# Router logits with the tokens as the stationary operand, in both mixtures of experts

## The reference

```python
# first mixture: 8 experts, top 2, and a gated shared expert
logits = jnp.einsum('bsh,eh->bse', x, gate_w)
probs = jax.nn.softmax(logits, axis=-1)
top_w, top_i = jax.lax.top_k(probs, K)
top_w = top_w / jnp.sum(top_w, axis=-1, keepdims=True)
...
shared_gate = jax.nn.sigmoid(x @ shared_gate_w)
...
# second mixture: 16 experts, top 6 of probs + gate_b
scores = xf @ gate_w.T
probs = jax.nn.softmax(scores.astype(jnp.float32), axis=-1)
biased = probs + gate_b
_, idx = jax.lax.top_k(biased, TOP_K)
```

## Time and profile before

| | |
|---|---|
| Time, median of 3 runs | 2141.92 us (2141.73 to 2150.73) |
| Span of the profiled execution, first to last instruction | 2139.0 us |
| Profiled execution's own time | 2139.0 us within its span; what lies around the span isn't shown |
| TensorE matmuls busy | 2077.7 us (97%), 12193 matmuls |
| VectorE busy | 1455.7 us (68%) |
| ScalarE busy | 1221.1 us (57%) |
| GpSimd busy | 576.8 us (27%) |

### The profile page before, as it was taken

How to read it: one execution, slowest core, us unless ns; L and a number is a source line. 1 busy time by engine, 2 the same in 40 slices (tenths; PEclk the granted TensorE clock), 3 DMA queues, 4 the chain that set the end, 5 groups by cost and what they waited for, 6 DMA issues and landing times. The chain is left out here.

```text
span 2139.0 us, 33422 instructions
## 1 busy us (share of the span) xinstructions
PE 2077.7 (97%) x12193; PEld 1588.5 (74%) x12193; DVE 1455.7 (68%) x2761; ACT 1221.1 (57%) x2435; POOL 576.8 (27%) x679
## 2 busy tenths in 40 slices
PE   8999999999999999989999999999999999999997
PEld 6888888888788888877777765333334688778886
DVE  5666666677667666666656567999994557655555
ACT  5666666666556666554444335888887434444433
POOL 3444444444334444332221110000000112222221
PEclk9999999999999999999999999999999999999999
DMA  2000000000000000011111202100000111111111
GB/s 75 20 21 18 16 21 21 21 21 21 9 21 21 21 21 20 4 38 45 38 44 40 56 22 44 24 19 22 21 12 1 43 37 45 45 45 45 45 52 57
DMA packets 55143, 64.67 MB, mean 30 GB/s; under 512 B 10268, under 2 KB 35655, under 8 KB 54983
## 3 DMA queue, kind: packets, MB, share of 16 engines
q1 hardware_dynamic: 54982, 62.55, 10.5%
HBM read 52.42 MB, written 2.10 MB: 25 GB/s over the span
## 5 line engine op out<-in xcount | busy, mean ns | idle before, releaser
L868 POOL TENSOR_TENSOR a_pr<-a_pr,a_rinv 128x512 f32<-128x512 f32 (+3 forms) x384 | 312.2, 827 | 474.7 <-DVE a_rinv L1118 474.7
L86 PE MATMUL psum<-xh,g_hi_gu 128*128 128x512 f32 x920 | 375.5, 408 | 7.8 <-DVE f_hid L1612 6.3
L88 PE MATMUL psum<-xh,g_lo_gu 128*128 128x512 f32 x920 | 359.8, 391 | 0.0
L87 PE MATMUL psum<-xl,g_hi_gu 128*128 128x512 f32 x920 | 359.2, 390 | 0.0
L1208 POOL TENSOR_TENSOR g_lo_gu<-g_raw_gu,g_hi_gu 128x512 fp32r<-128x512 f32 x84 | 108.8, 1295 | 758.5 <-ACT g_hi_gu L1204 758.5
L1926 ACT ACTIVATE a_pt<-psum 128x512 f32<-128x512 f32 x512 | 276.2, 597 | 59.2 <-PE psum L1826 37.9
L1945 DVE TENSOR_REDUCE x_m_negm<-psum 128x1 f32<-128x1024 f32 x240 | 290.8, 1224 | 13.5 <-PE psum L1811 11.2
L1546 ACT ACTIVATE f_act_s<-psum,g_gu_bias 128x512 f32<-128x512 f32 (+1 forms) x168 | 115.1, 685 | 295.5 <-PE psum L88 295.3
L1625 DVE TENSOR_TENSOR f_hl<-f_hid,f_hh 128x512 fp32r<-128x512 f32 x164 | 115.6, 705 | 226.3 <-ACT f_hh L1558 224.6
L1023 ACT ACTIVATE a_pr<-psum,a_negm 128x128 f32<-128x128 f32 (+7 forms) x256 | 190.1, 742 | 107.0 <-DVE a_negm L1108 102.9
L1030 ACT ACTIVATE a_pth<-psum 128x512 fp32r<-128x512 f32 (+3 forms) x384 | 174.7, 489 | 113.1 <-PE psum L927 107.7
(11 more groups left out here) (316 smaller groups left out, 4302.3 us busy)
## 6 DMA issues: line engine op xcount, KB each, us to landing
g_raw_gu<-in_gu SPq DMA_DIRECT2D x82, 256.0 KB, 2.8
f_raw_dn<-in_down SPq DMA_DIRECT2D x82, 128.0 KB, 2.0
g_raw_gu<-in_qkv SPq DMA_DIRECT2D x32, 256.0 KB, 2.8
a_wvr<-in_qkv SPq DMA_DIRECT2D x32, 128.0 KB, 2.4
a_wor<-in_o SPq DMA_DIRECT2D x32, 128.0 KB, 2.0
x_queries_qq<-x_qhi SPq DMA_DIRECT2D x128, 32.0 KB, 1.9
yT<-in_xT SPq DMA_DIRECT2D x4, 512.0 KB, 6.6
x_queries_qq<-x_qlo SPq DMA_DIRECT2D x64, 32.0 KB, 1.9
```

What stands on the lines that cost most here:

```text
L86: pe.matmul(out, a_hi, b_hi, start=first, stop=False)
L87: pe.matmul(out, a_hi, b_lo, start=False, stop=False)
L88: return pe.matmul(out, a_lo, b_hi, start=False, stop=last)
L868: pool.tensor_tensor(x, x, rinv[:, j:j + 1].to_broadcast([P, count * P]), ALU.mult).then_inc(p_done, 1)
```

## The change

The operands of `lg` are swapped: for each tile of 128 tokens the tokens are the stationary operand and the 10 or 16 columns of router weights move. The result has the tokens on the partitions, so the transposes of `lt`, its two copies' target in `yT` and the task itself go away. VectorE copies each `lg` task's four tiles straight into `lg`, and after the second it goes on with the maximum and the subtraction. The lists of tasks lose one entry for each router and, where slots are counted, the pause behind it.

```diff
     @staticmethod
     def has_bank(t):
-        return t[0] in ("lg", "lt", "ct", "cm")
+        return t[0] in ("lg", "ct", "cm")
...
+    def tile(self, n):
+        return slice(self.b * S + n * P, self.b * S + (n + 1) * P)
...
-            x = self.tokens(t[1])
-            for dt in range(DT):
-                i = mm3(pe, o[0:nr, :], rw.gwh[:, dt, :], rw.gwl[:, dt, :], self.xh[:, dt, x], self.xl[:, dt, x],
-                        dt == 0, dt == DT - 1)
-        elif kind == "lt":
-            pe.wait_ge(ring.emptied, ring.count((self.name, ("lg", 1))))
-            for n in range(self.TILES):
-                i = pe.transpose(o[:, n * nr:(n + 1) * nr], self.lgT[:, n * P:(n + 1) * P], self.ident[0:nr, 0:nr])
+            for q in range(CH // P):
+                x = self.tile(t[1] * (CH // P) + q)
+                for dt in range(DT):
+                    i = mm3(pe, o[:, q * nr:(q + 1) * nr], self.xh[:, dt, x], self.xl[:, dt, x], rw.gwh[:, dt, :],
+                            rw.gwl[:, dt, :], dt == 0, dt == DT - 1)
...
         if kind == "lg":
+            q0, nq = t[1] * (CH // P), CH // P
             dve.wait_ge(ring.filled, ring.count(key))
-            dve.tensor_copy(self.lgT[:, t[1] * CH:(t[1] + 1) * CH], ring.bank(key)[0:nr, :]).then_inc(ring.emptied, 1)
-        elif kind == "lt":
-            dve.wait_ge(ring.filled, ring.count(key))
-            dve.tensor_copy(self.lg[:], ring.bank(key)[:, 0:n * nr].rearrange("p (t n) -> p t n", n=nr)).then_inc(ring.emptied, 1)
+            dve.tensor_copy(self.lg[:, q0:q0 + nq, :],
+                            ring.bank(key)[:, 0:nq * nr].rearrange("p (t n) -> p t n", n=nr)).then_inc(ring.emptied, 1)
+            if q0 + nq < n:
+                return
...
-CHOOSE = [("lg", 0), ("lg", 1), ("lt",), ("ex",), ("pick",), ("weigh",)]
+CHOOSE = [("lg", 0), ("lg", 1), ("ex",), ("pick",), ("weigh",)]
...
-            return tasks(r, CHOOSE[:2]) + PAUSE + tasks(r, CHOOSE[2:3]) + PAUSE + tasks(r, CHOOSE[3:]) + PAUSE + maps(r)
+            return tasks(r, CHOOSE[:2]) + PAUSE + tasks(r, CHOOSE[2:]) + PAUSE + maps(r)
...
-                plan = {(0, 0): tasks(r1a, CHOOSE[2:4]), (0, 1): tasks(r1a, CHOOSE[4:5]), (1, 0): tasks(r1a, CHOOSE[5:]),
+                plan = {(0, 0): tasks(r1a, CHOOSE[2:3]), (0, 1): tasks(r1a, CHOOSE[3:4]), (1, 0): tasks(r1a, CHOOSE[4:]),
```

More of the change, by code:

```diff
@@ L302, in __init__ @@
         ne, nr, n = rw.ne, rw.nr, self.TILES
-        half = slice(b * S, (b + 1) * S)
-        self.lgT = yT[0:nr, 0, half]
         self.lg = ph.sb(f"{name}_lg", [P, n, nr])
```

## The result

The changed kernel took 2167.04 us in the median of 17 runs, the kernel before 2151.41 us in the median of 17 on the same chips, and the ratio is 1.0074 with a 95% interval of 1.0056 to 1.0093: 16 us slower, where I had forecast 6.8. Two things went wrong. The change costs more than twice what I took for the likeliest, and the kernel before is itself slower in the median than in the three runs that I started from, 2151.41 in place of 2141.92. Ratios leave out the few executions that lie far above the others of their kernel (2189.55 and 7020.72 us of the kernel before, 5254.22 in experiment 5, 9470.33 and 11421.12 in experiment 11), whose cause isn't known.

The account below looks back on a forecast made before the run. TensorE's queue was taken as the bound: 21.1 us of new logits replace 11.1 of old logits and 3.2 of transposes, +6.8; 2139.0 + 6.8 = 2145.8, with 2.9 around the span 2148.7 us; range 2145 to 2158.

Parts of the forecast that it names:

- The pace of the pair: Router logits on TensorE: one weight load with its narrow matmul takes 0.110 us, bounds 0.062 and 0.118.
- The added queue: TensorE at all four routers: 21.1 us in place of 14.3, so +6.8 us.
- Rival C: Router logits: load and matmul as quick as the transposes' pair, 0.062 us, 2.4 us gained, 2139.5 us; chance 0.06.
- The turning: The `lt` transposes of the logits, removed: 0.80 us of TensorE for each router, 3.2 us together.
- VectorE's relief: Smaller evictions and no `lt` copy: 1.2 us less on VectorE for each router, priced at nothing.
- Rival D: Waits, mainly behind `weigh` in the attention, absorb part of the cost: +3.3 us, 2145.2 us; chance 0.09.
- A: The main forecast: longer router tasks on TensorE add 6.8 us with the clock held, 2148.7 us; chance 0.49.
- B: TensorE's clock falls at the router tasks, two falls of 3.4 us each taken, 2155.5 us; chance 0.36.
- My row against B: At 2125 to 2130 us TensorE was busy 3.17 of 5.00 us, mostly transposes, and the clock stayed 1.00.
- The start of the sum: The profiled span of the kernel before, 2139.0 us, with 2.9 around it; median of the runs 2141.92.
- what the prediction left open beside it: Whether a weight load counts as activity that keeps TensorE's clock up; neither skill page nor trace showed it.

Follow-up runs that it names:

- experiment 5: The kernel before with swapped operands for the first attention's router (`r0a`) alone, its later tasks one spot earlier: ratio 1.0007 to the kernel before.
- experiment 11: The kernel before plus eight matmuls, results unread, in the first four steps of the second attention: ratio 0.9978 to the kernel before.
- experiment 12: The changed kernel plus eight matmuls, results unread, in the first four steps of the second attention: ratio 1.0056 to the kernel before.
- Experiments 1: The changed kernel with router weight columns repeated so each matmul moves 120 or 128 columns: 2161.03 us, ratio 1.0047 to the kernel before.
- 6: The kernel before with swapped operands for the router at the second mixture's head (`r1a`) alone, moving 128 columns: ratio 1.0000 to the kernel before.
- 7: The changed kernel with 120 or 128 moving columns and the old spots of `ex`, `pick` and `weigh`: ratio 1.0035 to the kernel before.
- experiment 2: The changed kernel with `ex`, `pick` and `weigh` put back in their old spots: 2159.66 us, ratio 1.0063 to the kernel before.

## Why the prediction was wrong

- **The pace of the pair** was right: 0.110 us taken, 0.11 seen, because the load sets it. The added queue is 6.5 us in place of 6.8, since a single task's matmuls start 0.108 us apart. Rival C fell with it.
- **The turning** was priced rightly at 0.80 us, and VectorE's relief at nothing. Rival D, 3.3 us in all, fell too: without the clock's part the change costs 5.7 us (+-0.9, experiment 12 over 11). Behind `weigh` the changed kernel waits 2.58 and 0.86 us where 1.71 and 0.80 were, so its waits didn't shrink. In experiment 5 alone the part without the clock is 0.7 us (+-1.0) for a queue of 1.6, so in the attention a little of it may be.
- **The step that failed** is the choice between A and B, "Forecast A, +6.8 us with the clock held, 0.49". The trace of before had no row that decided whether loads keep the clock up, and I gave the side without falls the larger chance. The runs showed falls in its place: in the profiled run 13.6 us at half clock in and right behind the narrow matmuls, and over all executions some 10 us lost to the clock beside 6 of queue. My row against B had no weight: the transposes of 2125 to 2130 us move 128 columns each, so they say nothing about matmuls that move 10. Experiments 1, 6 and 7 are at one with that, since there 120 or 128 columns were enough.
- **B's size.** I took two falls that cost 3.4 us each, 6.8 together. In the profiled run there are three at the router's matmuls, at 1020.1, 1695.9 and 1849.5, for 3.4, 6.8 and 3.4 us. That is 13.6 us at half clock and 6.8 us lost, as much as my two falls: 6.5 + 6.8 = 13.3 of the 16.3 us that this run has outside the long fall. The rest of its 16.3 are the falls behind `weigh` (603.7, 3.4 us long, 1.7 lost) and ahead of the router at the head (1685.7, 1.0 us added), which old-order kernels have too. So my 2155.5 for theory B, 11.5 us under the measured median, was low mainly by its start (9.5 us, the next point). How many come, and where, differs from run to run, as the falls at 572 and 586 in experiment 2 show. Over all executions the clock's part of the change is 10.1 us (+-2.4), more than one trace shows at the router's matmuls; which falls make up the rest isn't shown.
- **The start of the sum.** I took the profile of before for a typical execution. It was one of the quickest: of the 17 runs of before beside the result eleven lie above 2150 us. The profiles of the other kernels have, in places that the change doesn't touch, short falls near 540, 610, 1150 and 1210, and six of the ten others without the fill the long one from 1322 to 1330. The trace of before has none of them. In `e11_before_fill`, by stretch:

```profile
540.00:546.00 6.00, 5.49 (x17) 4.39 (x18) 1.79 (x6) 0.69 (x3) 0.61 (x1) 0.72 0.01 3
608.00:614.00 6.00, 4.36 (x12) 3.38 (x13) 3.22 (x10) 1.95 (x6) 0.84 (x2) 0.72 0.01 3
1150.00:1157.00 7.00, 5.78 (x21) 4.75 (x22) 3.86 (x12) 2.11 (x4) 0.73 (x1) 0.76 0.04 11
1208.00:1215.00 7.00, 5.21 (x14) 3.69 (x15) 3.98 (x4) 1.62 (x3) 1.10 (x2) 0.76 0.00 0
```

The three runs that I started from, one of them 9 us over the others, could have warned me.

- **The Trainium skill** (TensorE: Matmul & The Clock Gate, Part 4) says that transposes do not count as busy for the clock. I took the earlier trace rows to disagree with that, which went too far. The clock stayed up through the sixteen transposes at the end (2127.66 to 2129.6), but it fell at 2132.4, behind them, with TensorE idle from 2129.6 on:

```profile
2130.00:2132.40 2.40, 0.00 (x0) 0.00 (x0) 2.33 (x11) 1.68 (x2) 0.00 (x0) 0.99 0.00 0
2132.40:2139.00 6.60, 0.00 (x0) 0.00 (x0) 3.23 (x12) 0.30 (x1) 0.00 (x0) 0.50 0.47 159
```

The transposes at 1283.37 ran at half clock. So no row here speaks for or against the sentence. The stretch from 1015 to 1020 of the changed kernel answers what the prediction left open beside it: loads without many columns behind them didn't keep the clock up. (That loads can be pulled ahead of running matmuls stands in the table at the head of that page, not in the section that the prediction names.)

What stays open is what starts the short falls at 540 and behind `weigh`, why a single task brings a fall only in 10 cases of 24, and why the long fall lasts as it does. Experiment 5 was too blunt for the first.

## What to carry to other kernels

Swapping operands so that the thin side moves trades columns for weight loads, and with 128 stationary columns in fp32r a matmul cost 0.11 us, whether it moved 10 columns or 128. Count 128-column loads, not moved columns, and where a stream of narrow matmuls can't be avoided let it move more columns under the same loads: 120 columns took the time of 10, and the clock held in all 15 places of the traces. If two of the three products share an operand, putting the thin operands side by side saves whole passes: 3.8 us of queue here in the traces and 3.9 (+-0.7) in the part of the time without the clock, though the ratio alone (0.9983) isn't clear of 1. And before summing from one profile, look at the spread of the runs: a clock that falls in some executions is a term of the sum.

## What the runs showed of the hardware

- A TensorE that is never idle and loads weights almost without a break (4.60 of 5.00 us in 1015 to 1020) can lose its clock when 10 or 16 columns move with each load: behind 10 of 24 tasks of 2.6 us and in 4 of 4 runs of 48 matmuls. With 120 or 128 columns at the same pace of loads it kept the clock in 15 of 15.
- At half clock an fp32r pair of load and narrow matmul takes 0.21 us in place of 0.11, and the load is recorded with 333 ns in place of 192, so the load slows with the clock.
- The load of 128 columns in fp32r, recorded with 188 ns, repeats every 0.11 us, with 10 moving columns as with 128.
- A fall can last: in the second attention it took 24 to 34 us in six traces, over work that in others ran at full clock or lost it for 3.4 to 10.2 us. None of the three traces with eight more matmuls in the first four steps has a fall there. What holds it down that long isn't shown.
